# A gated cross-attention block with a routed expert layer: tile 0 from the first group's rows, another order at the start, scaling on ScalarE

## What is computed

```python
q = layernorm(x) @ wq + bq; k = ctx @ wk + bk; v = ctx @ wv + bv   # 16 heads of 16
score = einsum('bhqd,bhkd->bhqk', q, k) / 4 * mask
score = where(score == 0, -1e9, score)
x = x + tanh(g_xattn) * (merge(softmax(score) @ v) @ wo + bo)

xf = layernorm(x)                                   # 2048 tokens
probs = softmax(xf @ router_w + router_b)           # 4 experts
top_p, top_i = top_k(probs, 2); top_p /= top_p.sum(-1)
h = silu(xf @ w1[e]) * (xf @ w3[e])                 # 256 -> 1024
x = x + tanh(g_ffn) * sum_over_top2(top_p * (h @ w2[e]))
```

## Time and profile before

| | us |
|---|---|
| median of 3 runs | 521.58 (520.82 to 522.92) |
| profiled execution | 519.18 |
| its span, first to last instruction | 517.4 |

### The profile page before, as it was taken

One profiled execution on the slowest core, in us unless ns is written; L12 is line 12 of the kernel. 1 busy time (PEld: TensorE's weight loads), 2 busy tenths in 40 slices (PEclk: granted clock), 3 DMA queues, 4 the chain that ended last, 5 costly groups with the idle time before them and its releaser, 6 DMA issues.

```text
span 517.4 us, 11394 instructions
## 1 busy us (share of the span) xinstructions
PE 481.4 (93%) x3622; PEld 438.0 (85%) x3622; DVE 404.5 (78%) x955; ACT 305.1 (59%) x724; POOL 181.8 (35%) x190
## 2 busy tenths in 40 slices
PE   9989999999977899999999999999999999999991
PEld 7557787776756798999999999999999999998880
DVE  2598988998895488887788788888878888887660
ACT  3045556557445566686666656677666767776750
POOL 1456557368766017162036162022202210222111
PEclk9999999999999799999999999999999999999996
DMA  8999885001102302132013132022112111211110
GB/s 268 357 390 410 352 322 194 1 20 54 54 31 95 82 23 46 41 65 42 22 22 54 54 65 42 23 43 29 27 30 42 21 26 26 31 22 23 21 12 11
DMA packets 32392, 45.13 MB, mean 87 GB/s; under 512 B 9709, under 2 KB 28781, under 8 KB 32109
## 3 DMA queue, kind: packets, MB, share of 16 engines
q1 hardware_dynamic: 24807, 34.66, 19.5%
q0 software_dynamic: 6576, 8.92, 10.1%
q10 hardware_dynamic: 960, 0.94, 0.6%
HBM read 33.50 MB, written 21.82 MB: 107 GB/s over the span
## 4 chain that ended last, share of the span: by engine, by line
PE 41%; DVE 33%; issue 9%; POOL 6%; ACT 5%; DVEq 2%; DMA 1%; ACTq 0%; SPq 0%; POOLq 0%
PE ps_scores L1743 11%; DVE w_lo L1360 7%; PE ps_wide L1763 4%; DVE w_lo L1356 4%; DVE ps_scores L1365 3%; PE ps_misc L1763 3%; PE ps_probT L1743 3%; DVE hid_lo L1369 3%; PE ps_wide L1581 3%; ACT hid_hi L951 2%; PE ps_scores L1792 2%; DVE lowest L1235 2%; DVEq L688 2%; POOL score L1068 2%; DVE score L1224 2%
## 5 line engine op out<-in xcount | busy, mean ns | idle before, releaser
L1144 POOL DMA_INDIRECT out_x<-y_out,meta x35 | 57.0, 1627 | 207.5 <-DVE y_out L1388 202.4
L1360 DVE TENSOR_TENSOR w_lo<-w,w_hi 128x512 fp32r<-128x512 f32 x152 | 104.2, 686 | 15.4 <-ACT w_hi L930 7.9
L1743 PE MATMUL ps_scores<-xt_hi,w_hi 128*128 128x256 f32 x384 | 110.8, 289 | 0.2 <-DVE xt_lo L1374 0.2
L1743 PE MATMUL ps_scores<-xt_lo,w_hi 128*128 128x256 f32 x384 | 108.6, 283 | 0.0
L1743 PE MATMUL ps_scores<-xt_hi,w_lo 128*128 128x256 f32 x384 | 108.6, 283 | 0.0
L930 ACT CAST w_hi<-w 128x512 fp32r x152 | 95.3, 627 | 3.5 <-issue 3.0
L1743 PEld LDWEIGHTS ps_scores<-xt_hi,w_hi 128*128 128x128 f32 x384 | 73.5, 192 | 0.6 <-DVE xt_lo L1374 0.4
L1743 PEld LDWEIGHTS ps_scores<-xt_lo,w_hi 128*128 128x128 f32 x384 | 73.6, 192 | 0.0
L1743 PEld LDWEIGHTS ps_scores<-xt_hi,w_lo 128*128 128x128 f32 x384 | 73.5, 192 | 0.0
L951 ACT CAST hid_hi<-ps_scores 128x256 fp32r<-128x256 f32 x96 | 35.8, 373 | 57.5 <-DVE ps_scores L1365 56.1
L944 ACT ACTIVATE act_g<-ps_scores 128x256 f32<-128x256 f32 (+1 forms) x114 | 42.4, 372 | 21.9 <-PE ps_scores L1743 10.4
(11 more groups left out here) (236 smaller groups left out, 1221.1 us busy)
## 6 DMA issues: line engine op xcount, KB each, us to landing
grouped<-in_pad SPq DMA_DIRECT2D x1, 10296.0 KB
w<-in_L_ffn_w SPq DMA_DIRECT2D x8, 1024.0 KB, 12.9
w2s<-in_L_ffn_w SPq DMA_DIRECT2D x4, 1024.0 KB, 13.6
xg<-grouped SPq DMA_DIRECT2D x16, 256.0 KB, 2.7
out_x<-xall SPq DMA_DIRECT2D x8, 256.0 KB, 2.2
xall<-in_x SPq DMA_DIRECT2D x1, 1024.0 KB, 13.2
xall<-in_x SPq DMA_DIRECT2D x1, 768.0 KB, 7.5
ctxT<-in_ctx_t SPq DMA_DIRECT2D x2, 308.0 KB, 5.2
```

Of the source, the lines that this page charges most:

```text
L1144: pool.indirect_dma_start(out, bass.IndirectOffsetOnAxis(ap=meta[:, s % 2, t, E:E + 1].bitcast(U32), axis=0), y_out[:, s % 2, t, :], None, ...
L1360: dve.tensor_tensor(w_lo[:, f % NB], unit_weights(e, f), w_hi[:, f % NB].bitcast(F32), ALU.subtract).then_inc(w_lo_done, 1)
L1743: mm = pe.matmul(ps_gu[f % NB][:, m, 0:n], lhs, rhs[:, a, c, 0:n], start=(k == 0), stop=(k % (3 * DC) == 3 * DC - 1), skip_group_check=True)
```

## The change

- `FULL` also counts group 0: after its 1024 rows at least one tile must be full, so the first hand-out (0) gives out tile 0 alone, from group 0's rows, in batches 6 and 7 on DVE; hand-out 1 gives out tiles 1 to 4 at the end of batch 7, where the only one was; the one within tile 1 becomes number 2. All waits on counts move accordingly.
- SP loads tile 0's rows ahead of the output copy of batch 6, when hand-out 0 and group 0's scatters are through, and tile 1's ahead of the copy of batch 7.
- PE turns tile 0 ahead of `turn_ctx(7)` and the router product; ACT and DVE take its high and low half sooner; DVE's `logit` goes behind them.
- In batch 7, score tiles 2 and 3, `finish` goes ahead of `sink_zeros`, and `finish(7, 1)` ahead of the hand-out.
- At the start, the queries of batch 0 and its first scores go between the two halves of the values; scores, the turn and the queries of batch 1 go between the spreads; the spreads read 128 rows instead of 77 (the rest zero, cleared by GpSimd).
- `scale` goes from DVE to ACT, as two activations with the gate as their scale.

```diff
-FULL = [GB * SQ * TOP * (g + 1) // TILE - E + 1 for g in range(1, NG - 1)]
+FULL = [GB * SQ * TOP * (g + 1) // TILE - E + 1 for g in range(NG - 1)]
...
-            dve.wait_ge(ranked, i + 2)
+            dve.wait_ge(ranked, i + 1)
...
-                    if b == B - 1:
+                    if b >= B - 2:
+
+                        s = b - (B - 2)
                         sp.wait_ge(vals_done, 2)
-                        sp.wait_ge(handed, HAND)
-                        for k in range(GB):
-                            sp.wait_ge(scattered[k], 16 * TOP * GN)
-                        for s in range(2):
-                            r = sp.value_load(slot_start[0:1, s:s + 1], min_val=0, max_val=GROUPED_ROWS - TILE)
-                            sp.dma_start(xg[:, s], grouped[bass.ds(r, TILE), 0:D].rearrange("(t p) n -> p t n", p=P)).then_inc(x_in[s], 16)
+                        sp.wait_ge(handed, HAND * (s + 1))
+                        sp.wait_ge(scattered[s], 16 * TOP * GN)
+                        r = sp.value_load(slot_start[0:1, s:s + 1], min_val=0, max_val=GROUPED_ROWS - TILE)
+                        sp.dma_start(xg[:, s], grouped[bass.ds(r, TILE), 0:D].rearrange("(t p) n -> p t n", p=P)).then_inc(x_in[s], 16)
...
+                    for t in range(tiles_of(s)):
+                        gate_of = meta[:, a, t, bass.ds(e, 1)]
+                        act.activation(y_out[:, a, t], ps_y[a][:, t], ACT.Copy, scale=gate_of).then_inc(y_scaled, 1)
...
                 weights_hi(0, e, 0)
                 turned2_copy(act, NG - 2, 2, ps_scores[0][:, 0])
-                for f in range(1, AHEAD - 1):
+                x_hi(0, 0)
+                ctxT_copy(B - 1)
+                for f in range(1, AHEAD):
                     weights_hi(f, e, f)
-                ctxT_copy(B - 1)
-                x_hi(0, 0)
-                weights_hi(AHEAD - 1, e, AHEAD - 1)
...
+                pool.wait_ge(cleared, 2)
+                pool.memset(shared[P // 2:], 0.0).then_inc(cleared, 1)
...
+                        ends = b == B - 1 and s > 1
+                        if ends:
+
+                            finish(*((b, 0) if s == NS - 1 else (b - 1, s + 1)), False)
                         sink_zeros(b, s)
...
+                        if (b, s) == (B - 2, 0):
+                            hand_out(dve, 0)
+                        if (b, s) == (B - 2, 1):
+                            hand_out_begin(dve, 0)
+                            hand_out_owner(dve, 0)
+                        if (b, s) == (B - 1, 1):
+                            hand_out_rest(dve, 0)
...
+                values(0, 0)
+                values(0, 1)
+                mask_scores(0, 1, True)
+                values(1, 0)
+                sink_zeros(0, 1)
+                values(1, 1)
+                find_lowest(0, 1)
+                values(2, 0)
+                values(2, 1)
+                mask_scores(0, 2, True)
+                values(3, 0)
+                values(3, 1)
...
-                hand_out(dve, 0)
-                hand_out_begin(dve, 0)
                 finish(B - 1, 1, False)
+                hand_out(dve, 1)
+                hand_out_begin(dve, 1)
                 residual(B - 2)
-                hand_out_owner(dve, 0)
-                hand_out_rest(dve, 0)
                 finish(B - 1, 2, False)
+                hand_out_owner(dve, 1)
+                hand_out_rest(dve, 1)
                 finish(B - 1, 3, False)
-                logit(dve, NG - 2, ps_scores[1][:, 0])
...
-                for f in range(AHEAD - 1):
-                    weights_lo(f, e, f)
+                weights_lo(0, e, 0)
                 x_lo(0, 0)
+                logit(dve, NG - 2, ps_scores[1][:, 0])
+                weights_lo(1, e, 1)
                 residual(B - 1)
...
+                values(0, range(0, 2))
                 pe.wait_ge(ld_wq, 16)
                 project_q(0)
+                values(0, range(2, 4))
                 scores(0, 0, True)
+                pe.wait_ge(keys_copied, 2)
+                values(1, range(0, 4))
...
                 scores(0, 1, True)
-                for c in range(1, NC):
-                    for i in range(2):
-                        spread_v(c, i)
+                spread_v(1, 0)
+                spread_v(1, 1)
+                scores(0, 2, True)
+                spread_v(2, 0)
+                turn_x(1)
+                spread_v(2, 1)
+                scores(0, 3, True)
+                spread_v(3, 0)
+                spread_v(3, 1)
+                project_q(1)
+                spread_v(4, 0)
+                spread_v(4, 1)
...
-                turn_ctx(B - 1, True)
-                route_product(pe, NG - 2, ps_scores[1][:, 0])
...
                 turn_in(0, 0)
+                turn_ctx(B - 1, True)
+                route_product(pe, NG - 2, ps_scores[1][:, 0])
                 project_o(B - 1)
```

## The result

The changed kernel takes 514.61 us (median of 4 runs, 512.96 to 516.16), the kernel before 522.12 beside it: ratio 0.9858 with a 95% interval of 0.981 to 0.9906, so 7.5 us or 1.4% faster. Forecast were 513.3 us and 8.3 less; the time lies in the range. The terms of the sum fared very differently, though, and that is what the profile has to show.

The account below looks back on a forecast made before the run. It took PE and DVE to pace attention, GpSimd's scatters plus a load the handover, DVE stalls the early tiles, PE the late ones. Terms -6.8 + 1.6 + 0.9 - 3.6 - 0.4 = -8.3 gave 513.3 us, range 509.0 to 518.5.

Parts of the forecast that it names:

- hole: Between attention and experts: tile 0 loaded early, so PE no longer waits for scatters and load; -6.8 us, bounds 5.5 to 7.3.
- start, its order: Batch 0: matmuls moved among the spreads delay the last spread and first finish; +0.9 us, bounds -1.2 to +2.0.
- hand-out and finishes: Batches 6 and 7: 20 new DVE steps cost +2.0 and +1.1, finishing before zero-sinking gains about 1.5; together +1.6 us.
- granted clock in attention: Attention's PE clock: no term for a change, 0; the forecast read the clock only at the handover.
- early tiles, scaling: Expert tiles 1 to 7: scaling on ACT relieves DVE of stalls and a load; -3.6 us, bounds 1 to 6.
- late tiles: Later expert tiles: PE sets the pace, so scaling on ACT gains nothing; still 17.71 us per tile.
- short tiles and tail: Short expert tiles: 0.4 ahead of the product goes, three times, -0.4 us in all; the tail keeps its length.
- first expert matmul: Sign at the handover to experts: starts 3.5 to 5 us earlier, PE idle under 1 ahead, granted clock full.
- Rival B: Handover: SP's single queue loads tile 0 as late as before; sum only -1.5, 520.1 us, chance 0.05.
- Batch 7's last minimum: Sign at the end of attention: this DVE step comes about 4 us later than 155.25.
- Rival A: Batches 6 and 7: GpSimd blocks DVE, hand-out costs 7 or more, finishes gain nothing, start costs 2; 519.9 us, chance 0.10.
- rival C: Expert stage: ACT becomes the bound, each scaling changing tables and back at 1.28 each; 541 us, chance 0.03.

Follow-up runs that it names:

- e1: Changed kernel with the start order of the kernel before put back, the rest kept: 510.83 us, ratio 0.9777.
- e7: Changed kernel with 11 unused identity matmuls filling PE's waits in batch 0: 511.37 us, ratio 0.9809.
- e8: Changed kernel with the old start order and 16 unused identity matmuls in PE's waits in batches 6 and 7: 508.59 us, ratio 0.9749.
- e2: Kernel before with only the scaling of finished tiles moved from DVE to ACT: 515.45 us, ratio 0.9882.
- e5: Changed kernel with the old start order and the scaling back on DVE: 515.67 us, ratio 0.988.
- e9: Changed kernel with the old start order and each piece of the first hand-out ahead of its score tile's minimum: 508.12 us, ratio 0.9754.
- e12: Kernel before with nine unused identity matmuls filling PE's waits at its start: 519.93 us, ratio 0.9964.
- e3: Kernel before with 20 extra DVE hand-out steps, results unused, in the places of the new hand-out: 524.02 us, ratio 1.0041.

## Why the prediction was right, and where it was wrong

Against the profiled execution of before, in us (the ends of attention by the last piece of `turn2`):

| step | forecast | in the profiles | by runs of its own |
|---|---|---|---|
| hole | -6.8 | -6.9 | |
| start, its order | +0.9 | +0.95 | +3.8 with the clock (e1) |
| hand-out and finishes | +1.6 | +2.1 | |
| granted clock in attention | 0 | +6.6 | -3.2 (e7), -2.2 (e8) when filled |
| early tiles, scaling | -3.6 | -4.5 | -4.7 (e2, in its trace) |
| late tiles | 0 | 0.0 | |
| short tiles and tail | -0.4 | -1.4 | |
| sum | -8.3 | -3.2 | -7.5 between the medians |

Batch 7's mark is 4.0 later beyond the start (159.00 - 151.16 less 3.86). Of this 3.1 is the hand-out, as in e5, which has the same hand-out at full clock, and as in e7; 0.9 is the short stretch at half clock at 146.56. Finishing first gives back about 1: in e8 the mark is 3.9 later than in before and the last attend 2.9. The clock's line is then what is left of the 9.6: 2.9 behind the start, 0.9 in batch 6 and 2.8 in the closing chain.

**The hole** came out as worked: the turn at 172.65 without a wait, the projection at its full-clock time, the first expert matmul at its end. The first expert matmul nevertheless came 2.7 later and not 3.5 to 5 sooner, by what attention lost. One more number was off: xg[0] is issued at 158.16 on SP's queue, not loaded before 156, since everything ahead of it had slipped; it was still in time by over 10 us. xg[1] is issued at 174.94 and PE doesn't wait for it. Rival B fell.

**The start's order** was right to 0.1, with some luck: 34.2 and 5.3 of work make 39.5, not 39.1, and the measured 39.07 came about since the last copy ended at 34.07 and only 5.0 of work followed. What failed was the next step, which took the clock to be the same as before. The forecast did count the waits: the 0.5 that the first spread starts later, DVE's last copy near 34.2. It read the clock only in the hole, where 4.64 us of waiting stood ahead of it, and did not ask what waits of 0.5 to 1.7 us close together do. That term was missing for all three places, and it is the largest error of the sum, 6.6 us in this execution.

**The hand-out** cost the 3.1 put for it, but not where it was put. Batch 6's third minimum is 3.2 later (2.0 forecast), since each of its two pieces there was blocked once, 1.13 and 1.20, where one block was thought hidden. Batch 7's six steps, blocked for 1.08, should have added 1.1 and added nothing net, since the routing steps between the two minima got about as much shorter: from batch 6's third minimum to the end of the step `order` it is 5.8 us in before, with the 3.09 in it, and 4.4 in e5. So the sum was right by two errors that cancel. Batch 7's last minimum, forecast about 4 later than 155.25, ends at 162.56, 7.3 later; the 3.9 of the start are in that. The steps were put right behind the minima, where GpSimd is sure to begin. The Trainium skill (SBUF — State Buffer, Who interferes with whom) says that whichever of the two starts first holds the shared ports for its whole instruction. The trace agrees for these steps (1.20 on DVE at 133.55 beside GpSimd's 1.22 at 133.51). It does not for the step of 3.09 at 133.19 in the kernel before: that one began 0.6 ahead of GpSimd's subtraction and still ended with GpSimd's work. e9 shows what the forecast drew from it too late: part of the price, 1.0 of 3.1, hangs on where the steps stand against GpSimd's. Rival A, with its 7 and its 2 for the start, was nearer to the profiled execution than the forecast was, though 6.6 of the 9.6 were clock, which it had not named.

**The scaling** was undersized: each early tile gained 0.58 (turns of tiles 1 and 9 at 189.72 and 338.44, so 18.59 against 19.17), 4.65 between these turns and 4.5 counted from the first expert matmul, where 3.6 stood. ACT's price for the pair was right:

```profile
349.24 0.84 ACT L974 ACTIVATE y_out<-ps_wide,meta 128x256 f32<-128x256 f32 x2
```

0.84 against an estimate of 0.8. The late tiles stayed at 17.71. There is one table load in the expert stage, at 175.55, the one that was there before, so rival C fell. The stalls had been counted tile by tile as those right behind the scaling. PE's waits for hid_lo between tiles 1 and 9 went from 3.0 us to 0.5, and not all of them had stood behind a scaling. Where the rest of the gain lies was not taken apart: PE's idle time there fell by 2.6, its busy time by 1.7.

**Why the median fits all the same.** The forecast took 8.3 from the median of before. That median itself held some 2 us of low clock that its profiled execution did not have (e12: 1.8), and the changed kernel, with the hole gone, no longer hides what the closing chain loses but starts its experts at once. The scaling and the tail gave 1.9 more than forecast, which paid for part of it. So the 0.8 between 8.3 and 7.5 is small by luck: errors of several us on both sides cancel. The gain of the hole was right by its working, the scaling by its mechanism, with its size put too low.

## What to carry to other kernels

When an edit makes PE wait in pieces of 0.5 to 2 us in a part where it was nearly always busy, look at the clock behind them in more than one execution, and price it by the same instructions at either clock (1.30 and 2.40, 1.94 and 3.52 here). Filling such waits with matmuls that nobody reads tells cheaply whether the clock is the cause, and sometimes is the remedy. Put small DVE steps with two inputs ahead of the instruction that releases GpSimd, not behind it; it paid about 1 us for 20 steps here, by the marks. And a wait for a transfer hides slips of the work ahead of it: who removes it must count those slips in full. The best version measured is the changed kernel with the old start and the hand-out ahead of the minima, with or without the filling: 507.59 to 508.12 us, 0.9745 to 0.9754 of the kernel before.

## What the runs showed of the hardware

- In attention the granted clock fell to half (1.2 GHz) for 3 to 10 us behind waits of PE none of which was over 2.6 us, in parts where it was otherwise busy. The same place has it in one execution and not in another: around 29 us in the profiles of e2 and e3, not in those of before, e1 and e5, which share that start; behind waits of 1.37, 0.66 and 0.63 in after (146.56) and e1, not in e5 and e7, which have the same waits; behind a wait of 1.81 ahead of an attend in batch 7 in e12 (153.04), not in before, whose line stands below. Filling waits raised the mean clock (e7, e8), so the waits have a part in it, but they are not enough by themselves.

```profile
151.39 1.30 PE L1581 MATMUL ps_wide<-vblock,probT 128*128 128x68 f32 x10 [1.81 <-DVE ctxn L1253]
```

- A DVE step on four numbers a partition with two inputs from SBUF takes 0.16 us, and 0.6 to 1.2 beside a GpSimd instruction of that kind. Not stretched were, in after, the minimum at 132.65 (one input, 0.78 as ever, beside GpSimd's 0.71 at 132.32) and two-input steps beside GpSimd's issue of a scatter (130.38 and 130.57, 0.16 and 0.17, beside its 0.99 at 130.03). Two slow steps don't fit the picture: 3.09 at 133.19 in before and 0.55 at 128.04 in e9 began 0.6 and 0.5 ahead of GpSimd's instruction of that kind.
- ACT scales a 128x256 tile from PSUM by a number for each partition in 0.47 us, with no table change ahead of it.
